# A new timetable for the side work of a cross-attention kernel, and its second MLP matrix by 128 queries

## What is computed

```
q = layer_norm(Q) @ Wq + bq;  k = KV @ Wk + bk;  v = KV @ Wv + bv      # 16 heads of 16
attn = softmax(q @ k.T / sqrt(16));  ctx = attn @ v
x = Q + ctx @ Wo + bo
out = x + silu(layer_norm(x) @ W1 + b1) @ W2 + b2
```

## Time and profile before

| | us |
|---|---|
| median of 3 runs (lowest, highest) | 3684.07 (3683.93, 3684.78) |
| the profiled execution | 3687.68 |
| its span | 3685.9 |
| busy: PE, DVE, ACT, POOL | 3508.9, 2494.4, 2244.5, 929.4 |
| maxima reduces, 3328, mean | 2111.3, 0.665 |
| exponentials, 1664, mean | 1677.0, 1.024 |

### The profile page before, as it was taken

How to read it: one execution, slowest core, us unless ns; L and a number is a source line. 1 busy time by engine, 2 the same in 40 slices (tenths; PEclk the granted TensorE clock), 3 DMA queues, 4 the chain that set the end, 5 groups by cost and what they waited for, 6 DMA issues and landing times.

```text
span 3685.9 us, 52544 instructions
## 1 busy us (share of the span) xinstructions
PE 3508.9 (95%) x19620; PEld 1556.0 (42%) x19620; DVE 2494.4 (68%) x4643; ACT 2244.5 (61%) x2979; POOL 929.4 (25%) x1341
## 2 busy tenths in 40 slices
PE   5899999999999999999999999999999999999997
PEld 2333443444434444444444434444444444434435
DVE  5777767676676766767676676766767676676761
ACT  1466666656666566666656666566666656666564
POOL 1122314222231212313222231222313223132202
PEclk7999999999999999999999999999999999999998
DMA  4222212232121321212222122321213222122200
GB/s 95 60 40 39 49 30 53 42 65 40 25 52 35 66 42 33 51 32 58 42 59 38 28 52 39 66 39 35 46 33 63 42 42 50 30 52 42 42 7 12
DMA packets 121535, 162.96 MB, mean 44 GB/s; under 512 B 37040, under 2 KB 102592, under 8 KB 118208
## 3 DMA queue, kind: packets, MB, share of 16 engines
q1 hardware_dynamic: 120896, 159.40, 22.1%
q10 hardware_dynamic: 384, 0.20, 0.0%
HBM read 46.43 MB, written 8.39 MB: 15 GB/s over the span
## 4 chain that ended last, share of the span: by engine, by line
PE 80%; DVE 14%; ACT 3%; issue 2%; SPq 1%; DMA 0%; POOL 0%; ACTq 0%; DVEq 0%
PE o_ps L1171 20%; PE rows_ps L1137 19%; PE scores L1152 14%; DVE chunk_max L955 9%; PE side L1111 6%; PE side L1114 6%; PE side L1100 5%; PE side L1092 5%; PE side L1096 2%; PE side L1104 1%; ACT probs L803 1%; DVE stats L834 1%; DVE resid L861 1%; PE side L1107 0%; PE side L1086 0%
## 5 line engine op out<-in xcount | busy, mean ns | idle before, releaser
L955 DVE TENSOR_REDUCE chunk_max<-rows_ps 128x1 f32<-128x512 f32 (+1 forms) x3328 | 2111.3, 665 | 1052.7 <-PE rows_ps L1137 1044.3
L803 ACT ACTIVATE probs<-scores 128x1024 f32<-128x1024 f32 (+1 forms) x1664 | 1677.0, 1024 | 1136.7 <-PE scores L1152 1129.7
L1137 PE MATMUL rows_ps<-k_stack,q_stack 96*128 96x512 bf16 (+1 forms) x4096 | 1216.2, 339 | 97.1 <-DVE chunk_max L955 55.7
L1152 PE MATMUL scores<-q_stack,k_stack 99*128 99x512 bf16 (+1 forms) x3328 | 1037.2, 380 | 7.2 <-DMA q_stack<-shift_parts 4.2
L1171 PE MATMUL o_ps<-probs,v_sb 128*32 128x512 f32 x6656 | 886.4, 605 | 0.4 <-ACT probs L803 0.4
L1137 PEld LDWEIGHTS rows_ps<-k_stack,q_stack 96*128 96x128 bf16 x4096 | 332.0, 97 | 1191.0 <-DVE chunk_max L955 971.3
L1152 PEld LDWEIGHTS scores<-q_stack,k_stack 99*128 99x128 bf16 (+1 forms) x3328 | 324.8, 100 | 297.2 <-issue 37.3
L573 POOL TENSOR_TENSOR rest<-whole,k_parts 128x512 f32<-128x512 f32 x124 | 116.8, 942 | 969.8 <-ACT k_parts L748 965.4
L1111 PE MATMUL side<-hT,w_sb 128*128 128x256 f32 x968 | 259.8, 381 | 0.0
L1171 PEld LDWEIGHTS o_ps<-probs,v_sb 128*32 128x32 f32 x6656 | 130.9, 108 | 294.3 <-issue 220.4
L1100 PE MATMUL side<-wv_sb,ctxT 128*128 128x128 f32 (+1 forms) x1664 | 244.5, 279 | 7.3 <-DMA cf_c<-in_L_xattn_ln_ff_b 2.8
(11 more groups left out here) (107 smaller groups left out, 2049.5 us busy)
## 6 DMA issues: line engine op xcount, KB each, us to landing
k_stack<-k_parts SPq DMA_DIRECT2D x768, 50.0 KB, 2.2
k_stack<-k_stack SPq DMA_DIRECT2D x192, 200.1 KB, 5.6
ctx_nat<-in_ctx SPq DMA_DIRECT2D x47, 512.0 KB, 4.0
q_stack<-q_stack SPq DMA_DIRECT2D x192, 64.0 KB, 3.4
q_stack<-q_parts SPq DMA_DIRECT2D x756, 16.0 KB, 1.8
x_nat<-in_x SPq DMA_DIRECT2D x16, 512.0 KB, 6.1
resid<-in_x SPq DMA_DIRECT2D x32, 256.0 KB, 2.7
out<-resid SPq DMA_DIRECT2D x32, 256.0 KB, 2.5
```

What stands on the lines that cost most here:

```text
L803: nc.scalar.activation(probs[0:rows, (q + t) % 2, 2 * LQ * pair:2 * LQ * (pair + 1)], scores[0:rows, 2 * LQ * pair:2 * LQ * (pair + 1)], A ...
L955: nc.vector.tensor_reduce(dst, src, AX.X, ALU.max).then_inc(rows_read, 1)
L1137: last = nc.tensor.matmul(rows_ps[:, m % 2, d0:d0 + w], q_stack[s][0:STACK, h, P * t:P * (t + 1)], k_stack[s][0:STACK, h, k0:k0 + w], star ...
L1152: ins = nc.tensor.matmul(scores[0:keys_in(t), LQ * j:LQ * (j + 1)], k_stack[s][:, h, P * t:P * t + keys_in(t)], q_stack[s][:, h, :], start ...
```

## The change

The timetable is written anew: quarters get about the same side work, and steps go over two or three units. `v` half 1 (for the batch itself) stays in quarter 0 and half 0 in quarter 2, `k` half 0 in quarter 1, but `k` half 1 begins in quarter 2. Since a quarter can now prepare two halves, the table `PREPARED` goes, and each `k`, `v`, `q` step names its half (`half_of`, `batch_of`). `w2` becomes four steps of 128 queries, each with a sum of its own on VectorE. Besides, the inverted denominators are no longer copied to a wide tile before they are transposed; the transpose reads a broadcast view.

```diff
 PREPARE = (
-    [(0, 1, "v", 0), (2, 3, "v", 1), (4, 5, "v", 2), (11, 11, "v", 3)],
+    [(0, 2, "v", (1, 0)), (3, 5, "v", (1, 1)), (9, 11, "v", (1, 2)), (12, 12, "v", (1, 3))],
...
 FINISH = (
-    [(8, 9, "wo", 0), (18, 18, "h", 0), (20, 21, "wo", 1), (24, 24, "w1", (0, 0))],
+    [(6, 8, "wo", 0), (15, 15, "h", 0), (16, 17, "wo", 1), (18, 19, "w1", (0, 0)), (20, 21, "w1", (0, 1)),
+     (23, 24, "w1", (0, 2))],
...
+def half_of(kind, arg):
+
+    return arg if kind in ("k", "v") else (arg, 0) if kind == "q" else (None, arg)
+
+
+def batch_of(b, kind, arg):
+
+    return b - 1 if kind in FINISHING else b if kind == "v" and arg[0] == 1 else b + 1
...
-    first, second = {"turn": (QT, 1), "x": (QT, 1), "k": (1, KC), "q": (1, KC), "wo": (2, 2), "h": (KC, 2), "w1": (2, KC), "w2": (2, FM)}[kind]
+    first, second = {"turn": (QT, 1), "x": (QT, 1), "k": (1, KC), "q": (1, KC), "wo": (2, 2), "h": (KC, 2), "w1": (2, KC), "w2": (1, FM)}[kind]
...
+            def add_sum(kind, arg, sums):
+
+                if kind == "wo":
+                    dst, sums = resid[arg][:, :, :], sums[:, :].rearrange("p (t d) -> p t d", d=D)
+                else:
+                    dst, sums = resid[arg[0]][:, arg[1], :], sums[:, 0:D]
+                return nc.vector.tensor_tensor(dst, sums, dst, ALU.add)
...
-                    link(nc.vector.reciprocal(inverse[:, :], blocks[:, :, DH - q % 2]))
-                    link(nc.vector.tensor_copy(spread[:, :, DH:2 * DH],
-                                               inverse[:, :].unsqueeze(2).broadcast_to((P, LQ // 32, DH))))
-                    first = DH * (1 - q % 2)
-                    nc.vector.transpose(blocks, spread[:, :, first:first + 32]).then_inc(inverted, 1)
+                    link(nc.vector.reciprocal(inverse[:, :, 1], blocks[:, :, DH - q % 2]))
+                    first = 1 - q % 2
+                    nc.vector.transpose(denom[:, :].rearrange("p (c e r) -> p c e r", e=2, r=DH),
+                                        inverse[:, :, first:first + 2].unsqueeze(3).broadcast_to((P, LQ // 32, 2, DH)))\
+                        .then_inc(inverted, 1)
...
-                    ins = nc.tensor.matmul(side[:, D * i:D * (i + 1)], ffT_of[hf][:, j, P * i:P * (i + 1)], w2_sb[:, j, :],
+                    t = arg[1]
+                    ins = nc.tensor.matmul(side[:, 0:D], ffT_of[hf][:, j, P * t:P * (t + 1)], w2_sb[:, j, :],
                                            start=(j == 0), stop=(j == FM - 1))
```

More of the change, by code:

```diff
@@ L116 @@
 LATE = ([("wo", 0), ("wo", 1), ("h", 0)] + [("w1", (0, m)) for m in range(4)] + [("h", 1)]
-        + [("w1", (1, m)) for m in range(4)] + [("w2", 0), ("w2", 1)])
+        + [("w1", (1, m)) for m in range(4)] + [("w2", (hf, i)) for hf in range(2) for i in range(2)])
 LATE_ACT = [step for step in LATE if step[0] in ("h", "w1")]
@@ L149, in products_at @@
     for n, (first, last, kind, arg) in enumerate(steps):
-        todo, units = products(kind, arg), last - first + 1
+        todo, units = products(kind, half_of(kind, arg)[1]), last - first + 1
         for k, product in enumerate(todo):
@@ L293, in xattn_kernel @@
         denom = sb("denom", [P, LQ])
-        inverse = sb("inverse", [P, LQ // 32])
-        spread = sb("spread", [P, LQ // 32, 3 * DH])
+        inverse = sb("inverse", [P, LQ // 32, 3])
         attT = sb("attT", [P, 2, LQ])
@@ L631, in scale_group, with splits @@
                         .then_inc(att_ready, 1)
-            def splits(b, s, start, steps):
+            def splits(b, start, steps):
                 for k, (_, _, kind, arg) in enumerate(steps):
                     if kind in ("k", "q"):
-                        read_parts(b, s, start, k, arg if kind == "k" else NCH)
+                        s, c = half_of(kind, arg)
+                        read_parts(b, s, start, k, c if kind == "k" else NCH)
             def prologue():
@@ L656, in quarter @@
                 kinds = [step[2:] for step in steps]
-                ahead, s = PREPARED[q]
                 if q == 3:
-                    splits(b + ahead, s, start, steps)
+                    splits(b + 1, start, steps)
                 if q > 0:
@@ L806, in quarter @@
                     for k, kind, arg in at(steps, u):
[L807 to L810 removed]
+                        s, c = half_of(kind, arg)
+                        side_step(batch_of(b, kind, arg), s, start, k, kind, c)
             def epilogue(start):
@@ L971, in prologue @@
             def prologue():
-                nc.vector.memset(spread[:, :, :], 0.0)
+                nc.vector.memset(inverse[:, :, :], 0.0)
                 for stage in range(STAGES):
@@ L1032, in epilogue @@
                         late_silu(*arg)
-                for hf in range(2):
-                    late_sum("w2", hf)
+                for kind, arg in LATE_DVE[2:]:
+                    late_sum(kind, arg)
             walk(dve, prologue, quarter, epilogue, [(seq, DVE_SEQ_PER_BATCH)])
@@ L1046, in side_product @@
                 side = late_bank((kind, arg)) if late else side_bank
-                hf = 0 if not late else arg[0] if kind == "w1" else arg
+                hf = 0 if not late else arg[0] if kind in ("w1", "w2") else arg
                 if n == 0:
@@ L1218, in quarter @@
                         elif what == "side":
-                            kind = arg[1]
-                            if kind == "turn":
-                                side_product(per_quarter(1, bm, qm, 1), None, start, *arg)
-                            elif kind in ("wo", "h", "w1", "w2"):
-                                side_product(b - 1, None, start, *arg)
-                            else:
-                                side_product(b + ahead, s, start, *arg)
+                            k, kind, which, product, n, last = arg
+                            half, c = half_of(kind, which)
+                            b_of = per_quarter(1, bm, qm, 1) if kind == "turn" else batch_of(b, kind, which)
+                            side_product(b_of, half, start, k, kind, c, product, n, last)
                         elif u > 1:
```

51 lines of the change are left out of this document (20 added, 31 removed), and 8 rows, old and new, of tables (FINISH, PREPARE).

## The result

The changed kernel takes 3746.7 us (median of four runs, 3746.2 to 3747.7) against 3684.0. The ratio is 1.0169, with a 95% interval of 1.0157 to 1.0182: **slower by 62.7 us**, where 21 were forecast and 3742 was the upper end of the range. The sign was right, the size was not.

The account below looks back on a forecast made before the run. TensorE's work and waits set the batch: 222.4 us = 131.4 attention + 61.2 side work + 15.6 plain cost + 14.2 avoidable waits. Waits after 15.6, so +1.4 a batch, +20 over fourteen: 3705 us, range 3648 to 3742.

Parts of the forecast that it names:

- The sign: Whole kernel: the changed kernel was forecast slower than before, by 0.6%; slower by over 0.2% had chance 0.60.
- the five kinds of wait: TensorE's waits per batch after: ScalarE bank reads 7.5, VectorE sums 3.85, two-maxima tiles 1.55, light tiles 1.0, VectorE bursts 1.5 us.
- Part 2: Single side bank: a step's first product waits until ScalarE has read out the step before; 2.0 to 7.5 us a batch.
- the three behind the turn: Side-bank waits of `w1`, `w2` and `k`, which begin right after the turn step: 1.75 us a batch together.
- the three behind `v`: Side-bank waits of `v`, `h` and `w1`, each beginning right after a `v` step: 1.25 us a batch together.
- Part 3: Side bank read by VectorE: sums queue behind their unit's maxima, delaying the next step; 0.8 to 3.85 us a batch.
- Part 1: Levelling side work across quarters: fewer light tiles and tiles beginning with two maxima; gains 4.2 us a batch.
- double maxima: Tiles that begin with two maxima and carry side work: from ten to five, 3.1 to 1.55 us a batch.
- Part 4: VectorE bursts (statistics, inverse, silu, `v` tiles): waits fall from 4.6 to 1.5 us a batch, bounds 0.5 and 4.6.
- Part 5: Waits moved off the path: earlier `wo` 0 keeps 2 us of cover after GpSimd's attention product; no transfer delayed.
- Levelling wins: Faster rival: bank waits let VectorE catch up, partly replacing other waits; 3607 to 3648 us, typical 3650, chance 0.27.
- Slower still: Slower rival: VectorE's bursts stay at 4.6 us and the small sum costs 0.68; 3758 us, halfway 3731, chance 0.2.

Follow-up runs that it names:

- e4: Changed kernel with `q` 1 of quarter 3 in units 6-7 instead of 5-7: 3725.6 us against the changed kernel's 3746.7.
- e10: Changed kernel with the three steps behind the turn of unit 22 begun in unit 24 instead of 23: 3730.2 us.
- e5: Changed kernel, same steps in the same quarters, first and last units respaced so that a value product lies between steps where possible: 3602.4 us.
- e3: Changed kernel with `wo` and `w2` sums ahead of the maximum behind the value product in VectorE's order: 3703.0 us.
- e9: Kernel before, neither levelled nor split, only first and last units of steps respaced inside the quarters: 3636.9 us.
- e8: Changed kernel with the old timetable and split `w2`, whose steps start where `w2` started in the kernel before: 3735.6 us.
- e2: Kernel before with only the new inverse, transposed from a broadcast view without the copy: 3684.5 us, ratio 1.0002.

## Why the prediction came out as it did

**The accounting was right.** A batch repeats, the ends give about 1 us, and the five kinds of wait are the ones that the trace shows. The last step has a slip: 3707 less 3.6 is 3703, not 3705. It plays no part in what follows.

**Part 2 failed: "ready = end of the unit's scores + 0.93 + the step's read + 0.05".** It lets ScalarE start the moment TensorE is free of the product that it waits for; the timelines after show 0.2 us in between, and the whole record of the last of four operations, not their 0.36 pitch, ahead of TensorE. The trace of before had the 0.2 us too, a little ahead of the lines of the earlier trace rows:

```profile
1714.76 0.60 PE L1152 MATMUL scores<-q_stack,k_stack 99*128 99x512 bf16 x2
```

TensorE is through with these two at 1715.19 (the record ends at 1715.36, less the 0.38 of the second, plus 0.215), and the exponential of the earlier trace rows starts at 1715.39. Put into the formula, 1715.19 gives 1716.75 for the next `ctx`, 0.25 us after TensorE is free, where the row shows 0.45. Where a price was read off a row it held: four `ctx` exchanges at 1.9 forecast, 2.12 measured. Where it came from the formula it was short: the three behind the turn 1.75 against 2.45, the three behind `v` 1.25 against 1.73, `w1` (1,2) to `q` 0.9 against 1.27, `x` 1 to `q` 0.55 against 0.74. In all 7.5 against 9.6: 2.1 of the 3.05 us that the batch was off (226.85 against 223.8), 29 of the 42 us. So the formula, taken this way, missed the one row that it came from. e4 and e10 show that these exchanges are real and can be removed, e5 that most can. The records show that the 0.2 us is the rest of the product's own record and 0.03 to 0.04 us more; what lies behind either, no run shows.

**Part 3 held.** Sums 3.85 forecast, 4.0 measured; the 128x256 sum took 414 ns against 0.42 taken. e3 confirms the mechanism: with the sum moved, 3.0 us a batch go.

**Part 1 held in its direction.** Light tiles 0.75 against 1.0, double maxima 1.85 against 1.55. Waits for maxima fell by 113 us, and e5, 34 us faster than e9, is in line with a gain from levelling, though those two tables differ in the split too.

**Part 4 was too low,** 2.4 against 1.5, 13 us in all, within its bounds of 0.5 and 4.6. The silu of `w1` (1,3) two units ahead of `w2` was priced at 0.5 and cost a little over 0.6. The negation of the maxima in quarter 1, 0.63, had no price: the slower rival names those small operations (nine, it says; the trace has seven) and counts on 1.71 us of side work to cover them, where this tile carries one product of `q`, 0.86. e8 shows in another table how dear the negation is when a sum stands behind it.

**Part 5 held:** e2 shows the inverse at nothing, and no wait of `wo` on the attention product appeared.

**The rivals.** "Levelling wins" put its far end at 3607, and e5 reaches 3602, but by luck: e9 shows that spacing alone gives 46 of those 80 us. Its premise, that a bank wait hides VectorE's, is refuted by e3, and by e4 for ScalarE's. "Slower still" came nearest by its number (3758, halfway 3731), with the wrong parts: the sum was not dearer, the bursts took 0.9 of the 3.1 a batch that it gave them, and the larger part is in ScalarE's exchanges, which no rival varied. The range failed for that reason: it gave bounds to part 4 and to the sum, and none to the term of 7.5 us, half of the total, which rested mostly on a formula from one row.

**The rule on breaking up.** The Trainium skill, "Perfetto Trace Analysis", section "Optimizing Scalar/DVE Operations", has it that unsaturated engines which make others wait may finish sooner with smaller instructions. Here the sum did fall from 680 to 414 ns, and the kernel with the split `w2` in the old timetable is 53 us slower all the same (e1): each piece adds an exchange of the one bank, 1.8 of the 3.6 us a batch, and the rest is where the pieces were put. The place of a sum in the queue is worth 44 us (e3); its length was not varied by itself. The Trainium skill, same page, section "Optimizing Tensor Performance", asks for groups to rotate through banks. A second bank was not tried here, so no run shows what that gives; e5 puts time between the steps in its place.
